# A perceiver layer: sparse experts on tokens sorted through DRAM, and the router inside self-attention

## The reference

```
x = x + cross_attention(layernorm(x), ctx, ctx, mask)     # 16 heads, 257 keys per batch
x = x + self_attention(layernorm(x), Wq, Wk, Wv, Wo, ...) # 16 heads, 32 keys, decay mask
x = x + experts(layernorm(x), ...)

experts(xt):
  scores = xt @ gate_w                        # 8 experts
  ew, ei = top_k(scores, 2); ew = softmax(ew)
  wE[e, t] = ew where ei == e, otherwise 0
  h = gelu(xt @ w1[e] + b1[e])                # 128 -> 256
  o = h @ w2[e] + b2[e]                       # 256 -> 128
  y = layernorm(xt + o) * ln_g[e] + ln_b[e]
  out = sum over e of wE[e, t] * y[e, t]
```

## Time and profile before

| | |
|---|---|
| median of three runs | 933.85 us (933.37 to 934.37) |
| the profiled execution: its own time | 933.31 us |
| its span, first to last instruction | 931.4 us |
| mean granted clock of TensorE | 0.98 |
| PE busy | 804.2 us (86%) |
| DVE busy | 808.1 us (87%) |
| ACT busy | 636.4 us (68%) |
| POOL busy | 408.8 us (44%) |
| DMA | 27.6 MB, 30 GB/s on average |

### The profile page before, as it was taken

The page is one execution under the profiler, slowest core; times in us unless marked ns, Lnnn a source line. Parts: engine busy times, 40 slices in busy tenths (PEclk is TensorE's granted clock), DMA queues, the critical chain, the costliest instruction groups (busy, mean ns, idle before and its releaser), DMA issues. The chain is left out here.

```text
span 931.4 us, 32721 instructions
## 1 busy us (share of the span) xinstructions
PE 804.2 (86%) x10989; PEld 636.6 (68%) x10989; DVE 808.1 (87%) x2344; ACT 636.4 (68%) x2022; POOL 408.8 (44%) x420
## 2 busy tenths in 40 slices
PE   4898998899889889988669999979989898899882
PEld 2566666566666656665468888968878787788782
DVE  4888988988898889888659999957999999999994
ACT  3777777777777777777367777725767767776774
POOL 4222222322222222322114334344787777878785
PEclk9999999999999999999969999999999999999997
DMA  3221111111111111114000000000000000000000
GB/s 89 70 84 40 51 37 51 37 48 44 40 51 37 51 37 51 40 41 164 7 2 2 3 2 3 4 1 1 8 6 6 11 6 6 6 11 6 6 10 14
DMA packets 32717, 27.60 MB, mean 30 GB/s; under 512 B 3548, under 2 KB 32408, under 8 KB 32664
## 3 DMA queue, kind: packets, MB, share of 16 engines
q1 hardware_dynamic: 32664, 26.87, 9.8%
HBM read 24.76 MB, written 2.10 MB: 29 GB/s over the span
## 5 line engine op out<-in xcount | busy, mean ns | idle before, releaser
L544 ACT ACTIVATE E<-SC,neg_max 128x257 f32<-128x257 f32 x512 | 235.9, 474 | 101.8 <-DVE neg_max L604 101.8
L604 DVE TENSOR_REDUCE neg_max<-SC 128x1 f32<-128x257 f32 x512 | 181.9, 417 | 36.7 <-PE SC L401 34.1
L414 PE MATMUL ETP<-ident,E 128*128 128x128 f32 x1024 | 162.3, 286 | 37.9 <-ACT E L544 37.4
L613 DVE TENSOR_TENSOR Et<-ETP,mask_T 128x512 f32<-128x512 f32 x256 | 172.5, 684 | 15.5 <-PE ETP L414 14.4
L414 PEld LDWEIGHTS ETP<-ident,E 128*128 128x128 f32 x1024 | 108.8, 142 | 88.5 <-issue 78.4
L1311 PE MATMUL PO<-W,hid 128*128 128x128 f32 x1024 | 137.9, 278 | 18.7 <-ACT hid L1352 18.7
L1376 ACT ACTIVATE Y<-Z,zb,zs 128x128 f32<-128x128 f32 x256 | 111.0, 485 | 60.1 <-DVE zb L1531 60.1
L1311 PEld LDWEIGHTS PO<-W,hid 128*128 128x128 f32 x1024 | 131.2, 192 | 28.9 <-issue 21.5
L1300 PE MATMUL PH<-xT,W 128*128 128x256 f32 x512 | 135.4, 387 | 0.5 <-ACT xT L1344 0.5
L1352 ACT ACTIVATE hid<-PH,b1c 128x256 f32<-128x256 f32 x256 | 105.5, 463 | 19.3 <-PE PH L1300 17.8
L544 ACT ACTIVATION_READ_ACCUMULATOR E<-SC,neg_max 128x1 f32 x512 | 103.8, 203 | 0.0
(11 more groups left out here) (161 smaller groups left out, 1406.3 us busy)
## 6 DMA issues: line engine op xcount, KB each, us to landing
V<-in_ctx_dram SPq DMA_DIRECT2D x64, 256.0 KB, 2.6
xh<-in_x_dram SPq DMA_DIRECT2D x32, 64.0 KB, 2.2
last_rep<-in_ctx_dram SPq DMA_DIRECT2D x128, 2.0 KB
X<-in_x_dram SPq DMA_DIRECT2D x32, 64.0 KB
out_dram<-Xo SPq DMA_DIRECT2D x64, 32.0 KB, 1.5
W<-in_L_ffn_w_dram SPq DMA_DIRECT2D x1, 1024.0 KB
W<-in_L_ffn_w_dram SPq DMA_DIRECT2D x2, 512.0 KB
b2r<-in_L_ffn_b_dram SPq DMA_DIRECT2D x1, 512.0 KB
```

Of the source, the lines that this page charges most:

```text
L414: i = pe.transpose(ETP[s][:, c:c + P], E[:, j // HB, NQ * (j % HB) + 2 * s + u, k * P:(k + 1) * P], ident[:, :])
L544: i = act.activation(E[:, h, at, :], SC[:, u, 0:S], ACT.Exp, bias=neg_max[:, j % 2, u:u + 1], accum_out=den[:, h, at:at + 1])
L604: dve.tensor_reduce(neg_max[:, j % 2, u:u + 1], SC[:, u, 0:S], AX.X, ALU.max, negate=True).then_inc(max_sb, 1)
L613: dve.tensor_tensor(Et[:, 2 * (j % 2) + s, :, :, :].rearrange("p u k c -> p (u k c)"), ETP[s][:, :], mask_T[:, :, :, :].rearrange("p u k c ...
```

## The change

The third stage computes only the two chosen experts of each token, and the first two stages prepare it.

- **Cross-attention.** SP also writes empty rows into a DRAM tensor `slots` of 65 blocks of 256 rows of 130 floats (`fill`, 8 blocks, 1.06 MB, for each tile). W1 is no longer loaded as a whole. POOL and DVE set a few more constants.
- **Self-attention.** The decay of half 0 is put into PSUM by a matmul with the identity (`put_decay`) and the `add_decay` of half 0 goes. In the bodies lies the router: for each tile the second layernorm (`route_stats`, `route_mean`, `route_var`, `route_power`, `route_norm`), a transpose and the gates on PE (`route_turn`, `route_gates`); for each two tiles 13 small DVE operations that choose two experts, a set of matmuls that count (`ranks`), and 10 small DVE operations that give each token its row in `slots` and its weight. POOL then sends the normalised rows with their weight and their own number to `slots`, 4 indirect DMAs of 128 rows for each tile (`send`). There are 22 bodies. After them DVE makes the table of blocks (`list_blocks`).
- **Experts.** 39 blocks of 256 rows, each of one expert. SP loads the block from `slots` and its W1 from DRAM, at an address that it reads from the table (`value_load`); PE, ACT and DVE read the expert's number in the same way. Per block: transpose, `first`, `gelu`, `second`, `collect`, `stats`, `means`, `scaled`, `gained`, now on two groups of 128 rows. `inverse` is one pow on POOL for two blocks. POOL scatters the result with two indirect DMAs into the DRAM tensor `parts`. Before the blocks, the bias ln_b times the weights is added to X (`turn_weights`, `mix_bias`, `biased`). After them all of `parts` is loaded again, DVE adds both parts of each token and X, and SP and ACT store the result.

```diff
+NBLK = (2 * TOKENS + NE * (BLK - 1)) // BLK      # 39
...
                         load_ctx(sp, t, 3)
+                        fill(8 * t, 8)
...
-                sp.dma_start(W1[:, :, :], w1.rearrange("e c f -> c e f")).then_inc(w3_in, 16)
+                sp.wait_ge(empty_set, 3)
+                fill(8 * (T - 1), 8)
+                fill(0, 8)
+                fill(SPARE, 1)
...
+                def route_norm(u):
+                    dve.wait_ge(r_rs, u + 1)
+                    xt = tile_of(u)
+                    for e in range(2):
+                        i = dve.tensor_scalar(XN[:, u, e, :, 0:D], xt[:, e * D:(e + 1) * D].unsqueeze(1).to_broadcast([P, 2, D]),
+                                              rmv[:, e, 0:1], rrs[:, e:e + 1], ALU.subtract, ALU.mult)
+                    i.then_inc(r_xn, 1)
...
                 def body(t):          # DVE
+                    now, soon, behind = t < T, t + 3 < T, 1 <= t <= T
+                    choosing, k = t % 2 == 1 and 5 <= t <= T + 3, (t - 5) // 2
+                    seating, n = t % 2 == 0 and 6 <= t <= T + 4, (t - 6) // 2
+                    if 0 <= t - 3 < T:
+                        route_norm(t - 3)
+                    if now:
+                        maxima(t, 0)
                     if t + 2 < T:
                         norm(t + 2)
-                        add_decay(t, 0)
-                        maxima(t, 0)
-                        add_decay(t, 1)
+                    if 0 <= t - 4 < T:
+                        keep_gates(t - 4)
...
                 def body(t):          # POOL
-                    if 2 <= t:
+                    if 0 <= t - 2 < T:
                         bias(t - 2)
+                    if 0 <= t - 6 < T:
+                        send(t - 6, 0)
                     if t < T:
                         normalise(t, 0)
                         if t + 3 < T:
                             power(t + 3)
                         normalise(t, 1)
+                    if 0 <= t - 2 < T:
+                        route_power(t - 2)
+                    if 0 <= t - 6 < T:
+                        send(t - 6, 1)
...
+                def put_decay(t):
+                    if later(t):
+                        pe.wait_ge(d_sb, 2 * t - 1)
+                    pe.matmul(PS[0][:, :, :].rearrange("p u s -> p (u s)"), ident[:, :], decay[:, :, :].rearrange("p u s -> p (u s)"),
+                              start=True, stop=False, skip_group_check=True)
...
+            load_weights(0)
+            sp.wait_ge(sent, 16 * 4 * T)
+            for i in range(NBLK):
+                if i >= NX:
+                    wait_gone(sp, i - NX)
+                n = sp.value_load(table[0:1, 0, i:i + 1], min_val=0, max_val=SPARE)
+                sp.dma_start(XS[:, i % NX, :, :].rearrange("p e c -> p (e c)"),
+                             slots[bass.ds(n, 1), :, :].rearrange("n (p e) c -> p (n e c)", e=2)).then_inc(xs_in[i % NX], 16)
+                if i + 1 < NBLK:
+                    load_weights(i + 1)
...
+            for i in range(NBLK + 3):          # POOL
+                if i % 2 == 0 and 2 <= i <= NBLK + 1:
+                    inverse(i // 2 - 1)
+                if i >= 3:
+                    send(i - 3)
...
+                for i in range(NBLK + 3):      # DVE
+                    if i < NBLK:
+                        collect(i)
+                    if i % 2 == 0 and 2 <= i <= NBLK + 1:
+                        factors(i // 2 - 1)
+                    if i + 1 < NBLK:
+                        b2, gain[i + 1] = expert(i + 1)
+                        spread(i + 1, b2)
+                    if i % 2 == 0 and 2 <= i <= NBLK + 1:
+                        factors2(i // 2 - 1)
+                    if i < NBLK:
+                        stats(i)
+                    if i >= 3:
+                        gained(i - 3, gain[i - 3])
+                    if i < NBLK:
+                        means(i)
+                    if i < NBLK and (i % 2 == 1 or i == NBLK - 1):
+                        variance(i // 2)
```

More of the change, by code:

```diff
@@ L741, in attend @@
         W, hh_wide, decay, out_bias, bcol, bq_own, neg_half, Kbd = consts
+        (G, w3_in, before_me, all_ones, count_f, rev, home, start_of, steps16, up_to, filled, sent, XN, wt, table, slots, past_sems) = routes
+        rstat = sb("rstat", [P, 2, 6])
+        rmv = sb("rmv", [P, 2, 2])
+        rvar = sb("rvar", [P, 2])
+        rrs = sb("rrs", [P, 2])
+        xT3 = sb("xT3", [P, 2 * P])
+        gs = sb("gs", [P, 2 * T, NE])
+        best = sb("best", [P, 2, GB])
+        same = sb("same", [P, GB, NE])
+        ranked = sb("ranked", [P, GB, NE])
+        lead = sb("lead", [P, GB])
+        rest = sb("rest", [P, GB, NE])
+        hot = sb("hot", [P, GB, 2, NE])
+        taken = sb("taken", [P, GB, NE])
+        gap = sb("gap", [P, GB])
+        ratio = sb("ratio", [P, GB])
+        total = sb("total", [P, GB])
+        share = sb("share", [P, GB, 2])
+        parted = sb("parted", [P, GB, 2, NE])
+        seat = sb("seat", [P, GB, NE])
+        seats = sb("seats", [P, GB, 2, NE])
+        place = sb("place", [P, GB, 2])
+        place_i = sb("place_i", [P, T, 2, 2], I32)
+        dest_i = sb("dest_i", [P, T, 2, 2], I32)
+        count = sb("count", [1, NE])
+        over = sb("over", [1, NE, PER])
+        blocks = sb("blocks", [1, NE])
+        below = sb("below", [1, NE, NE])
+        ends = sb("ends", [1, NE])
+        past = sb("past", [1, NTAB, NE])
+        past_end = sb("past_end", [1, NTAB, NE])
+        owner = sb("owner", [1, NTAB])
+        begun = sb("begun", [1, NTAB])
+        where = sb("where", [1, NTAB])
         stat = sb("stat2", [P, 2, 6])
@@ L1156, in mix_experts @@
[L1156 to L1171 removed]
+        w1, W2, b1c, b2r, gr, b_rows, neg_half, wt, table, sent, slots, parts = consts
@@ L1250, in _, with inverse @@
-            power(0)
-            pool.wait_ge(w_in, W_DMAS)
-            for p in range(NP):
-                spread(0, p)
-            run(slots, pool)
-            inverse(T - 1, 1)
-            finish(T - 2)
-            for p in range(1, NP):
-                gather(T - 1, p)
-            finish(T - 1)
+            def inverse(p):
+                n = pair(p)[1]
+                pool.wait_ge(z_v, p + 1)
+                if p >= 2:
+                    pool.wait_ge(z_s, p - 1)
+                pool.tensor_tensor(zr[:, p % 2, 0:n, :].rearrange("p n e -> p (n e)"), zv[:, p % 2, 0:n, :].rearrange("p n e -> p (n e)"),
+                                   neg_half[:, 0:2 * n], ALU.pow).then_inc(z_r, 1)
@@ new lines, in first, with second @@
+            def first(i):
+                pe.wait_ge(xt_sb, i + 1)
+                pe.wait_ge(w1_in[i % NW], 16 * (i // NW + 1))
+                if i >= 2:
+                    pe.wait_ge(h_sb, i - 1)
+                for a in range(FH):
+                    pe.matmul(PH(i, a), W1[:, i % NW, a * P:(a + 1) * P], xT[:, i % 2, :], start=True, stop=True).then_inc(h_ps, 1)
+            def second(i, w2):
+                pe.wait_ge(h_sb, i + 1)
+                if i >= 2:
+                    pe.wait_ge(z_sb, i - 1)
@@ new lines, in expert @@
+            def expert(i):
+                e = pe.value_load(table[0:1, 1, i:i + 1], min_val=0, max_val=NE - 1)
+                return W2[:, bass.ds(e, 1), :, :].rearrange("p n a d -> p (n a d)")
+            turn_weights()
+            mix_bias()
+            pe.wait_ge(x_b, T)
+            turn(0)
+            w2 = expert(0)
+            for i in range(NBLK + 1):
+                if i < NBLK:
+                    first(i)
+                    if i + 1 < NBLK:
+                        turn(i + 1)
+                if i > 0:
+                    second(i - 1, before)
+                before = w2
+                if i + 1 < NBLK:
+                    w2 = expert(i + 1)
@@ new lines, in scaled, with expert @@
+            def scaled(i):
+                act.wait_ge(z_b, i // 2 + 1)
+                if i >= 2:
+                    act.wait_ge(u_sb, i - 1)
+                for e in range(2):
+                    m = act.activation(Y[:, i % 2, e, :], Z[:, i % NY, e, :], ACT.Identity, scale=zs[:, i % 4, e:e + 1],
+                                       bias=zb[:, i % 4, e:e + 1])
+                m.then_inc(y_sb, 1)
+            def expert(i):
+                e = act.value_load(table[0:1, 1, i:i + 1], min_val=0, max_val=NE - 1)
+                return b1c[:, bass.ds(e * FH, FH)]
@@ new lines, in result @@
+            def result(c):
+                dve.wait_ge(y_sum, c + 1)
+                dve.tensor_tensor(YB[:, 0, 2 * c:2 * c + 2, :], YB[:, 0, 2 * c:2 * c + 2, :], X[:, 2 * c:2 * c + 2, :],
+                                  ALU.add).then_inc(x3, 1)
+            for t in range(T):
+                biased(t)
+            blocks()
+            dve.wait_ge(x_b, T)
+            both(0)
+            for c in range(T // 2):
+                if c + 1 < T // 2:
+                    both(c + 1)
+                result(c)
```

1005 lines of the change are left out of this document (557 added, 448 removed).

## The result

The changed kernel takes 1003.39 us (median of 4 runs, 1002.07 to 1009.71) against 933.93 us for the kernel before on the same chip: ratio 1.0757, 95% interval 1.0711 to 1.0804. It is 7.6% slower; 856 us was forecast, and no end of the forecast's range (790 to 915) holds it. The profiled execution has a span of 1002.7 us.

What follows compares the result with a forecast made beforehand. DVE was to bound self-attention, ending at 684 us, and POOL the blocks, 39 times 3.2 us, to 824; drain 9 and end 20 gave 853, small additions 856 us, against 933.85; range 790 to 915.

Steps and rivals of the forecast that it cites:

- With the coupling of five queues 3.2 us, 39 times: Experts' blocks: POOL the largest at 3.1 us, 3.2 per block with coupling, 124.8 us in all; lowest 2.3, highest 4.4.
- Drain of the blocks: Experts, end: the last block drains through the whole chain and the landing of its scatter, 9 us.
- End of self-attention: Bodies 183.1 us from 474.2, then 6.1, a bare router chain 9.8 and 8 DMAs 10.4: ends at 683.6 us.
- The price of a body: Self-attention: with DVE full, about 12 us for a full body (10.8 to 13.5), 183.1 us for all bodies.
- the prediction's own sign of being wrong: Self-attention: the forecast is wrong if PE rather than DVE paces the bodies.
- again 6.1: Self-attention, end: the last tile takes 6.1 us after the last body, the same as before the change.
- The stage's end: Barrier after self-attention: the stage goes from 683.6 us to 684 with the barrier.
- Filling the pipeline: Experts, ahead of the steady blocks: filling the pipeline takes 4 us, steady from 699 us.
- an indirect DMA: POOL, self-attention and blocks: 1.3 us each, taken from nearby rows because the trace has no such DMA.
- All four cases: Forecast 856 us, chance 0.59; cheaper queues 804 us, 0.19; scatter bounds the blocks 904 us, 0.12; slower 989 us, 0.10.
- the slower rival: `send` and block scatters: POOL can't write addresses while DVE runs, 2.6 us per DMA, 989 us; chance 0.10.
- the figure of 3.1 us beside a DVE copy: Skill page on SBUF: a DMA issued from GpSimd takes 0.62 us alone, 3.1 us beside a DVE copy.

Runs made afterwards that it cites:

- the two versions with open rings: Kernel after with factors ahead of collect, 16 XS buffers, and either two blocks more lag (893.15 us) or pow ahead of scatters and scaled, gained, scatters one step later (894.62).
- the version with both rings open: Kernel after with factors, scaled, gained and scatters two blocks later, 16 XS buffers, and factors ahead of the next collect: 893.15 us, 0.9586 of the kernel before.
- the version with 16 buffers: Kernel after with factors, scaled, gained and scatters two blocks later and XS with 16 buffers in place of 8: 918.06 us, 0.9842 of the kernel before.

## Why the prediction was wrong

- **The step that failed: "With the coupling of five queues 3.2 us, 39 times".** The block was priced as the work of the fullest engine, 3.1 us, and 0.1 us for the coupling. POOL's term was right: two indirect DMAs and half a pow measure 3.1 us, and the two versions with open rings run at 3.4. But whether the queues could lie beside each other was never asked. Written out, the orders show it: on ACT `scaled(i-2)` ahead of `gelu(i+1)`, on POOL two scatters ahead of the pow, on DVE the factors behind `collect(i)`. Following one wait around gives a ring of 12.4 us a pair. Worth 111 us (235.7 against 124.8 for all blocks), shown by reordering and by lag: the version with both rings open has 3.4 us a block and takes 110 us less. Up to 25 us of it come by TensorE's low clock, which the waits bring with them.
- **Drain of the blocks**: 9 forecast, 19 measured (961.5 to the first loads of the parts at 980.6), +10. In the trace the last block's pow stands behind four scatters on POOL, 5.3 us after its input was ready (966.73 to 972.05), and four more scatters come behind it:

```profile
966.56 0.17 DVE L1822 TENSOR_SCALAR zv<-zmv 128x2 f32<-128x2 f32 x1
...
972.05 0.75 POOL L1654 TENSOR_TENSOR zr<-zv,neg_half 128x2 f32<-128x2 f32 x1
```

- **End of self-attention**: forecast 683.6. The last addition ended at 676.4, not 663.4 (+13). Of this 7 us had come by the start of body 15 (652.6), as a full body takes 13.0 us and not 12. The price of a body rested on a full DVE, and that failed: DVE is 80% busy from 540 to 650 us, PE 91%, and DVE waits for PE more than for POOL. This comes near to the prediction's own sign of being wrong, that PE paces the bodies; no run tests it. The other 6 us lie behind that start: the term "again 6.1" took the bodies after the last tile as unchanged, while parts of the router of the last tiles now stand in them. Behind the addition not 8 sends but 16 trailed (682.1 to 702.1, at 1.27 us each; +5.5): POOL sent almost without a pause from 662 to 675 us, and the last two pairs of tiles get their row numbers 7.3 us apart where a pair's sends take 10.2. Together +18.5; the tail of 16 sends is shown by the runs, the rest is read from the trace alone.
- **The stage's end**: 0.4 forecast, 5.6 measured, +5.
- **Filling the pipeline**: 4 forecast, 7.4 measured (718.4 to 725.8), +3.
- **Cross-attention** (+0.5 forecast, +0.4 measured, fills hidden), **an indirect DMA** (1.3 forecast, 1.27 to 1.29 from start to start), **ahead of the blocks** (11, measured 10.7) and **the end** (20, measured 22) were right. DVE is idle for 0.26 to 0.9 us, 0.5 on average, where it reads a register, a little under the 0.7 assumed.
- Added up: 18.5 + 5 + 3 + 111 + 10 + 2 = 149.5, and 1002.7 - 853.6 = 149.1.
- **The rivals.** All four cases priced engines, and none a ring. That the result lies near the slower rival's 989 is no credit to it: its price was 2.6 us per DMA, and a DMA costs 1.3. Nor did the figure of 3.1 us beside a DVE copy, which the prediction drew from the Trainium skill ("SBUF — State Buffer", the section on the two sides of SBUF), show itself: in the rows above none of 78 scatters took over 1.16 us and none of 64 sends over 1.22, though DVE was 80% busy beside the sends. Whether any of DVE's operations there is a copy of the kind that the page measured, no run here tells.

## What to carry to other kernels

Where a change splits work into blocks that pass five in-order queues, write down each queue's order and follow one wait around before adding up busy times: an instruction that waits for this block's result and stands ahead of the next block's work closes a ring, and the block then costs the ring's length. Here the block came down to the work of the fullest engine only where three things were done together: the waiting instruction behind the next block's work, what releases it not behind a wait of its own, and buffers for every block in flight. One alone left or uncovered another ring, and lag without buffers made the time 15% worse. An idle of several us on all engines with one releaser each is how a ring looks in a profile.

## What the runs showed of the hardware

- After an indirect DMA from POOL, the end of a stage waits: 5.6 us from the end of the last one to the next stage's first matmul (702.1 to 707.7; 697.6 to 703.2 in the version with 16 buffers), but 0.3 us where the last one lay 11 us back. An ordinary POOL operation as the last one brings no such wait: at the end of cross-attention in the kernel before, POOL's ends at 459.09 and DVE goes on at 459.45. The wait is longer than such a DMA's landing, 2.2 us as the median of the blocks' scatters, and the DMA engines move nothing from 703.0 to 707.5; what is waited for isn't shown.
- An indirect DMA of 128 rows costs POOL 0.96 to 1.0 us (medians; the longest 1.26 in all kernels) and 0.30 between two, in self-attention with 520-byte rows as in the blocks with 512-byte ones.
- TensorE's granted clock, on average over the blocks: 0.74 in the kernel after, 0.55 with more lag and 8 buffers, 0.94 with both rings open, 0.99 with matmuls that nobody reads in the wait. In one pair of the kernel after it stood at 0.50, the lower level, from 812.0 to 816.3 us, behind 6.9 us without a matmul.
